# A fixed rotation of the score and probability buffers that is the same in every batch

## The reference

```python
xn = layernorm(x)                       # twice, the second with ln_w and ln_b
q, k, v = proj(xn, Wq, bq), proj(xn, Wk, bk), proj(xn, Wv, bv)   # 16 heads of 16
q, k = rope(q), rope(k)
scores = einsum('bhqd,bhkd->bhqk', q, k) / sqrt(16)
out = einsum('bhqk,bhkd->bhqd', softmax(scores), v)
x + out @ Wo.T + bo
```

## Time and profile before

| | us |
|---|---|
| median of three executions | 1780.56 |
| the profiled execution's own time | 1778.8 |
| its span, first to last instruction | 1777.0 |
| eight batches of attention (about 75 to 1187) | 1112 |
| expert layer (about 1187 to 1777) | 590 |
| PE busy | 1678.4 (94%) |
| PE weight loads busy | 973.7 (55%) |
| ACT busy | 1201.4 (68%) |
| DVE busy | 1035.3 (58%) |

### The profile page before, as it was taken

The page is one execution under the profiler, slowest core; times in us unless marked ns, Lnnn a source line. Parts: engine busy times, 40 slices in busy tenths (PEclk is TensorE's granted clock), DMA queues, the critical chain, the costliest instruction groups (busy, mean ns, idle before and its releaser), DMA issues.

```text
span 1777.0 us, 28942 instructions
## 1 busy us (share of the span) xinstructions
PE 1678.4 (94%) x11240; PEld 973.7 (55%) x11240; DVE 1035.3 (58%) x2056; ACT 1201.4 (68%) x1416; POOL 508.4 (29%) x480
## 2 busy tenths in 40 slices
PE   4499999999999999999999998889999999999997
PEld 4233344434434434434434443348888888888886
DVE  8655457556557557547647648847555454555543
ACT  3498888898898898898888889973333333333322
POOL 2101201111111111112110110025565656565653
PEclk9699999999999999999999999999999999999998
DMA  3634566558458456465475465535443434444332
GB/s 115 189 58 91 152 115 132 126 127 156 105 126 158 118 135 138 115 142 111 116 164 113 103 147 101 103 101 130 96 102 54 100 56 101 89 66 90 64 55 30
DMA packets 113459, 195.03 MB, mean 110 GB/s; under 512 B 20881, under 2 KB 59153, under 8 KB 113297
## 3 DMA queue, kind: packets, MB, share of 16 engines
q1 hardware_dynamic: 84112, 142.48, 36.2%
q0 software_dynamic: 29184, 50.35, 14.8%
HBM read 116.22 MB, written 76.55 MB: 108 GB/s over the span
## 4 chain that ended last, share of the span: by engine, by line
PE 90%; DVE 4%; ACT 4%; issue 1%; DMA 1%; POOL 0%; SPq 0%; ACTq 0%; DVEq 0%; POOLq 0%
PE o_ps L958 26%; PE score L1025 20%; PE score L944 19%; PE side L831 5%; PE score L1037 5%; ACT probs L748 3%; PE o_ps L1037 3%; PE side L872 3%; PE side L841 3%; PE side L1037 2%; PE side L815 2%; PE score L1012 1%; DVE rot L1174 1%; DVE stats L1073 0%; PE side L822 0%
## 5 line engine op out<-in xcount | busy, mean ns | idle before, releaser
L748 ACT ACTIVATE probs<-score 128x1024 f32<-128x1024 f32 x1024 | 978.1, 1027 | 141.9 <-PE score L944 141.9
L958 PE MATMUL o_ps<-probs,v_ones 128*32 128x512 f32 x4096 | 493.8, 600 | 0.7 <-DVE o_sb L1369 0.7
L944 PE MATMUL score<-q_stack,k_stack 50*128 50x512 f32 x2048 | 398.1, 456 | 43.3 <-ACT probs L748 34.9
L944 PEld LDWEIGHTS score<-q_stack,k_stack 50*128 50x128 f32 x2048 | 164.1, 185 | 356.4 <-ACT probs L748 296.3
L732 ACT ACTIVATE probs<-score 128x512 f32<-128x512 f32 x128 | 76.6, 599 | 335.8 <-PE score L1025 335.7
L659 POOL DMA_INDIRECT out<-probs,rot x128 | 204.3, 1596 | 212.2 <-DVE probs L1332 182.9
L958 PEld LDWEIGHTS o_ps<-probs,v_ones 128*32 128x32 f32 x4096 | 106.4, 108 | 231.2 <-issue 151.0
L1317 DVE TENSOR_TENSOR probs<-score,probs 128x512 f32<-128x512 f32 x128 | 88.6, 692 | 209.4 <-PE score L1025 181.8
L637 POOL TENSOR_TENSOR square<-qk 128x512 bf16<-128x512 f32 x56 | 77.2, 1407 | 400.4 <-DVE qk L1180 400.4
L1025 PE MATMUL score<-parts,q_stack 128*128 128x512 f32 x640 | 158.2, 389 | 0.0
L648 POOL DMA_INDIRECT qk<-xn_rows,rot x128 | 133.4, 1043 | 38.4 <-issue 29.3
(11 more groups left out here) (247 smaller groups left out, 2556.4 us busy)
## 6 DMA issues: line engine op xcount, KB each, us to landing
q_parts<-parts SPq DMA_DIRECT2D x16, 1024.0 KB, 4.3
k_parts<-parts SPq DMA_DIRECT2D x16, 1024.0 KB, 7.3
q_stack<-q_parts SPq DMA_DIRECT2D x62, 256.0 KB, 7.3
k_stack<-k_parts SPq DMA_DIRECT2D x62, 256.0 KB, 9.4
q_stack<-q_parts SPq DMA_DIRECT2D x66, 128.0 KB, 8.1
k_stack<-k_parts SPq DMA_DIRECT2D x66, 128.0 KB, 8.9
o_sums<-o_sb SPq DMA_DIRECT2D x256, 32.0 KB
num<-o_sums SPq DMA_DIRECT2D x32, 256.0 KB
```

The source lines that it names most:

```text
L748: act.activation(probs[probs_of(b, s)][:, 2 * i:2 * i + 2, :], score[ring_of(b, p)][:, :, :], ACT.Exp, scale=SCALE).then_inc(exp_done, 1)
L944: last = pe.matmul(score[ring_of(b, p)][:, w, :], k_stack[par][rows, i, kt * P:(kt + 1) * P], q_stack[par][rows, i, qh * HALF:(qh + 1) * H ...
L958: last = pe.matmul(o_ps[j * KEYS_W:(j + 1) * KEYS_W, :], v_ones[par][:, kt, j, :], probs[probs_of(b, s)][:, j, :], start=kt == 0, stop=kt ...
```

## The change

Both functions lose their argument b: a pair or a step now lies in the same buffer in every batch. `ring_of(p)` is p mod 3 for every p from 0 to 127 (126 lies in `score0`, 127 in `score1`). Since the next batch begins with `score0` again, its pairs 0 and 1 follow at a distance of two, and its pair 2 at a distance of five. For the steps, `probs_of(s)` is s mod 3 up to step 50, step 51 is put into `probs1`, and step 52 begins again with `probs0`, so that step 63 ends in `probs2` and the border of the batch is even. The distance is two steps at steps 51 and 53, four at 52 and 54, and three elsewhere. `pairs_since` and `steps_since` compute these distances, and the waits use them.

```diff
-    assert (NB * PAIRS - 1) % RING == 0
+    EXTRA_STEP = 51
+    assert EXTRA_STEP % 3 == 0 and (STEPS - 1 - EXTRA_STEP) % 3 == 0 and (PAIRS - 2) % RING == 0
...
-    def ring_of(b, p):
-
-        return (b * PAIRS + p + 1) % RING
-
-    def probs_of(b, s):
-
-        return (b * STEPS + s) % PROBS
+    def ring_of(p):
+
+        return p % RING if p < PAIRS - 2 else p - (PAIRS - 2)
+
+    def pairs_since(p):
+
+        return next(n for n in range(1, PAIRS) if ring_of((p - n) % PAIRS) == ring_of(p))
+
+    def probs_of(s):
+
+        return s % 3 if s < EXTRA_STEP else 1 if s == EXTRA_STEP else (s - EXTRA_STEP - 1) % 3
+
+    def steps_since(s):
+
+        return next(n for n in range(1, STEPS) if probs_of((s - n) % STEPS) == probs_of(s))
...
-                need(act, pv_done, at - PROBS + 1)
+                need(act, pv_done, at - steps_since(s) + 1)
...
-                need(pe, exp_done, b * PAIRS + (p - RING + 1))
+                need(pe, exp_done, b * PAIRS + (p - pairs_since(p) + 1))
```

More of the change, by code:

```diff
@@ L747, in attend @@
                     act.wait_ge(qk_done, b * PAIRS + p + 1)
-                    act.activation(probs[probs_of(b, s)][:, 2 * i:2 * i + 2, :], score[ring_of(b, p)][:, :, :], ACT.Exp,
+                    act.activation(probs[probs_of(s)][:, 2 * i:2 * i + 2, :], score[ring_of(p)][:, :, :], ACT.Exp,
                                    scale=SCALE).then_inc(exp_done, 1)
@@ L940, in scores @@
                 p = NPAIR * s + i
-                need(pe, exp_done, b * PAIRS + (p - RING + 1))
+                need(pe, exp_done, b * PAIRS + (p - pairs_since(p) + 1))
                 for w in range(LANES):
                     rows = slice(w * LANE, w * LANE + FULL)
-                    last = pe.matmul(score[ring_of(b, p)][:, w, :], k_stack[par][rows, i, kt * P:(kt + 1) * P],
+                    last = pe.matmul(score[ring_of(p)][:, w, :], k_stack[par][rows, i, kt * P:(kt + 1) * P],
                                      q_stack[par][rows, i, qh * HALF:(qh + 1) * HALF],
@@ L958, in weigh @@
                 last = pe.matmul(o_ps[j * KEYS_W:(j + 1) * KEYS_W, :], v_ones[par][:, kt, j, :],
-                                 probs[probs_of(b, s)][:, j, :], start=kt == 0, stop=kt == KT - 1)
+                                 probs[probs_of(s)][:, j, :], start=kt == 0, stop=kt == KT - 1)
             last.then_inc(pv_done, 1)
```

## The result

The changed kernel took 1790.86 us (median of four executions, 1789.08 to 1792.96), the kernel before 1780.07 us (four, 1778.8 to 1781.35). The ratio is 1.0061, with a 95% interval of 1.0043 to 1.0079: slower by 10.8 us or 0.6%. I had forecast slower by 6.1 us, with a range up to 1789.4 us, and the time lies above it. The direction and the first mechanism were right; a second one was missing. The profiled execution took 1791.6 us with a span of 1789.8, 12.8 us over before's 1777.0.

The account below looks back on a forecast made before the run. The loop over PE and ACT was taken as the bound, PE alone in cycles with a long job. Terms of 6.4 - 0.3 + 0 = 6.1 us on the median 1780.56 gave 1786.7 us, range 1783.8 to 1789.4.

Parts of the forecast that it names:

- The bound: Attention: a loop over PE and ACT, 3.96 us a cycle without a job; PE alone in cycles with a long job.
- Term 1: Score buffers at seven batch borders: pair 1 waits one exponential more, 0.915 us each, 6.4 us in all.
- pair 0 hidden: At the borders, pair 0's later start is covered by ACT's own work, with 0.16 us to spare.
- The work queued behind pair 1: At each border, PE's products of steps 62 and 63 keep their 1.85 us and begin 0.915 us later.
- Term 2: Behind border 3, PE's lateness absorbs its wait for DVE's copy of `o_ps`: -0.3 us, bounds 0 to 0.7.
- Term 3: Probability buffers, steps 51 and 53 of eight batches: the shorter distance costs 0, at most 1.6 us.
- PE catches up: Behind the borders, PE's headroom gives the 0.915 us back: 1780.6 us; 1 in 10 together with the DVE case.
- DVE's copy never ended last: Opposite claimed: copy last by 0.9 us at all seven borders hides the delay, 1780.6 us; 1 in 10 with PE catching up.
- Pair 2's looser wait: At the borders, the longer distance removes 0.84 us before pair 2's loads: 5.9 us gained, 1774.7 us; 3 in 100.
- ACT didn't stall at steps 51 and 53: Opposite claimed: ACT waits 0.93 us more for products at 16 places, 14.8 us on top, 1801.5 us; 3 in 100.

Follow-up runs that it names:

- e3: Kernel before, with pair 1's wait at each of the seven borders counting one exponential more (127 in place of 126); ratio 1.0066 against the kernel before.
- e6: Changed kernel plus two unused float32 products on PE at each border, ahead of pair 0 and of pair 1; ratio 1.0041 against the kernel before.

## Why the prediction was partly right

*The bound* was read rightly: the loop over PE and ACT carries every delay to the end. e3 and e6 show it, where a wait of 0.91 us at seven places makes over 6 us. Nor is the delay given back within a batch: the copies of `o_ps` are 0.95 us late against the kernel before's ahead of border 1, 1.85 us behind it, and still 1.81 us at the last one ahead of border 2.

*Term 1, the price of a border* was right: 0.915 us forecast, 0.91 to 0.92 measured at the four borders where the clock held, pair 0 hidden, pair 1 at 1.99 us.

*The work queued behind pair 1* is the step that failed, and with it the multiplication of one price by seven. The sentence "so none of the 1.85 us gets shorter or runs ahead: they begin 0.915 us later" took over the 1.85 us of before for the products, and had no case in which they get longer. At three of seven borders they took 3.20 to 3.41 us, since TensorE's clock had fallen to half, and ACT stood idle for 2.73 to 2.75 us in place of 1.10. The sum lacked these 3 x 1.63 = 4.9 us. e6 shows the cause: with PE busy in the same wait the falls are gone and the 0.9 us a border stay. The signs that I had: PE's idle time in the loop is 0.71 us in one piece, the change puts 0.94 and 0.41 us with a pair between them in its place, and the clock was 1.00 in every stretch I had looked at in attention. I took a constant for granted where only PE's work before had kept it so, and named no rival in which an idle PE gets slower.

*Term 2* was right in kind and size: ACT's idle time one cycle behind border 3 is 0.47 us in the kernel before and 0.19 in the changed kernel, and also in e6, where the clock held there. *Term 3* was right: 0.9997 for the probability buffers alone.

*The rivals.* That PE catches up is refuted: the delay of each border is still there at the next. The Trainium skill, "Perfetto Trace Analysis", section "Identifying the Most-Contended Engine", has TensorE's headroom judged by the share of its weight loads; I had worked out from its 42% that a delay could be made up, and that does not hold in this loop over two engines. DVE's copy never ended last at the changed kernel's borders: PE's only wait for it in attention is one of 0.54 us, in the last batch. Pair 2's looser wait gained nothing, and ACT didn't stall at steps 51 and 53.

My range was built from the spread of the executions and the terms' bounds, all at one clock speed; it left out the one term of the other kind.

## What to carry to other kernels

A buffer that comes back one turn earlier costs what is queued behind the wait, once for each time, if the engines are tied in a loop; moving work that doesn't depend on it ahead of the wait makes it free. When a wait makes TensorE idle, price the work behind it at both clock levels, and count how often the idle stretch occurs. Cutting TensorE's work into alternating pieces to fill a wait pays only where it really waits: each cut costs it here about 0.1 to 0.2 us.

## What was not expected of the hardware

The clock fell at some borders and not at others with the same instructions and the same idle time, by one profile each: at 3, 5 and 7 in the changed kernel, at 1, 3, 5 and 7 with its score buffers alone, at 3 and 5 with pair 1's wait alone. PE's 0.94 us of idle time in one piece (pair 0's wait alone) brought no fall, 0.94 and 0.41 us close together did at three of seven, 1.63 us in one piece at two of seven, and 2.16 us (border 1) to 2.55 us at all seven. Each fall made the products behind the wait take 2.8 to 3.6 us in place of 1.85. What decides between two alike borders stays open; neither PE's busy time ahead of the fall nor the DMA traffic does in the changed kernel.
